# The hidden layer of a two-layer graph network: its up product as seven half-width products per pair of hidden blocks

## The reference, cut to what matters

```python
h = maximum(layernorm(x), 0);  x = x + L0_gnn_ref(h, W, src, dst, edge_weight)
h = maximum(layernorm(x), 0)
# second layer
h  = h + segment_sum(h[src], dst)            # N x 256
h1 = h @ W1 + b1                             # N x 1024, the "up product"
h1 = relu((h1 - mean) * rsqrt(var + 1e-5) * gamma + beta)
out = relu(h1 @ W2 + b2)                     # N x 256, the "down product"
x = x + out
```

## Time and profile before

| | |
|---|---|
| median of 3 runs | 3866.1 us (3864.36 to 3868.13) |
| the profiled execution: its own time | 3856.75 us |
| its span | 3854.9 us |
| TensorE, busy over the span | 3418.6 us, 17,108 matmuls |
| VectorE | 2279.5 us, 5,133 instructions |
| ScalarE | 2125.0 us, 3,435 instructions |
| GpSimd | 1155.8 us, 899 instructions |
| first up matmul of the node stage | at 1665.7 us |
| one full chunk of the node stage | 22.31 us |

### The profile page before, as it was taken

One profiled execution on the slowest core, in us unless ns is written; L12 is line 12 of the kernel. 1 busy time (PEld: TensorE's weight loads), 2 busy tenths in 40 slices (PEclk: granted clock), 3 DMA queues, 4 the chain that ended last, 5 costly groups with the idle time before them and its releaser, 6 DMA issues.

```text
span 3854.9 us, 57297 instructions
## 1 busy us (share of the span) xinstructions
PE 3418.6 (89%) x17108; PEld 2899.8 (75%) x17108; DVE 2279.5 (59%) x5133; ACT 2125.0 (55%) x3435; POOL 1155.8 (30%) x899
## 2 busy tenths in 40 slices
PE   0378887587877879999999999999999999999999
PEld 0367777576766657778888888888888888888888
DVE  0356665576565579955555555555555555555555
ACT  0255555323222279956666666666666666666665
POOL 6667777688888744400000000000000000000000
PEclk9888988788888889999999999999999999999999
DMA  9988877577777799933433433433333343343342
GB/s 343 338 201 192 191 191 141 140 169 163 157 161 154 169 319 378 363 120 113 125 116 111 125 118 109 124 121 109 121 124 109 116 129 109 115 130 109 114 125 69
DMA packets 305855, 619.83 MB, mean 161 GB/s; under 512 B 34997, under 2 KB 186800, under 8 KB 299856
## 3 DMA queue, kind: packets, MB, share of 16 engines
q1 hardware_dynamic: 229440, 515.46, 40.4%
q0 software_dynamic: 75264, 102.81, 15.6%
q10 hardware_dynamic: 1072, 0.76, 0.1%
...
## 4 chain that ended last, share of the span: by engine, by line
PE 63%; POOL 19%; DMA 8%; issue 7%; DVE 1%; ACT 1%; POOLq 0%; DVEq 0%; SPq 0%; ACTq 0%
PE ps_a L1303 28%; PE ps_b L1317 19%; PE ps_b L1318 10%; POOL x_table L554 7%; POOL agg_table L554 7%; POOL edge_tiles L544 4%; DMA x_table<-in_x 4%; PE ps_a L1261 3%; PE ps_a L1263 2%; DMA x_table<-edge_tiles,scatter_now 2%; PE ps_a L1262 2%; DMA agg_table<-edge_tiles,scatter_now 1%; POOL edge_ring L544 1%; DVE late_r L1039 0%; DMA edge_tiles<-x_table,gather_ids 0%
## 5 line engine op out<-in xcount | busy, mean ns | idle before, releaser
L1317 PE MATMUL ps_b<-w_hl,late_r 128*128 128x512 f32 x3128 | 1129.2, 397 | 0.0
L1145 DVE TENSOR_TENSOR late_r<-hid,late_r 128x512 fp32r<-128x512 f32 (+1 forms) x784 | 537.4, 685 | 813.6 <-ACT late_r L767 813.6
L762 ACT ACTIVATE hid<-ps_a,bn_bias,bn_scale 128x512 f32<-128x512 f32 (+1 forms) x784 | 608.8, 777 | 733.9 <-PE ps_a L1303 733.9
L1303 PE MATMUL ps_a<-late_r,w_hi 128*128 128x512 f32 x3136 | 983.5, 395 | 0.0
L1318 PE MATMUL ps_b<-w_hl,late_r 128*128 128x256 f32 x3128 | 877.6, 281 | 0.0
L1317 PEld LDWEIGHTS ps_b<-w_hl,late_r 128*128 128x128 f32 x3128 | 588.1, 188 | 137.9 <-issue 0.5
L1303 PEld LDWEIGHTS ps_a<-late_r,w_hi 128*128 128x128 f32 x3136 | 540.4, 188 | 107.9
L1303 PE MATMUL ps_a<-late_r,w_lo 128*128 128x512 f32 x1568 | 612.3, 390 | 0.0
L1318 PEld LDWEIGHTS ps_b<-w_hl,late_r 128*128 128x128 f32 x3128 | 591.2, 189 | 26.3
L767 ACT ACTIVATE late_r<-hid 128x512 fp32r<-128x512 f32 (+1 forms) x784 | 494.8, 631 | 71.7
L1231 PE MATMUL ps_b<-edge_tiles,edge_same 128*128 128x256 f32 x1568 | 408.2, 426 | 0.0
...
## 6 DMA issues: line engine op xcount, KB each, us to landing
x_rows<-x_table SPq DMA_DIRECT2D x291, 512.0 KB, 4.4
late<-agg_table SPq DMA_DIRECT2D x194, 512.0 KB, 5.8
...
hT_f<-hT_table SPq DMA_DIRECT2D x97, 512.0 KB, 3.7
out<-zeros SPq DMA_DIRECT2D x97, 512.0 KB, 6.7
...
```

The lines of the kernel that those rows point to most:

```text
L762: act.activation(hid[m % 2][:, 0:w].rearrange("p (r a b) -> p r a b", a=BANDS, b=SQUARE), by_row, ACT.Relu, scale=bn_scale[:, m:m + 1], bi ...
L1145: dve.tensor_tensor(hid_lo[m % 4][:, 0:w], hid[m % 2][:, 0:w], hid_hi[m % 4][:, 0:w].bitcast(F32), ALU.subtract).then_inc(hid_lo_ready, 1)
L1303: ins = pe.matmul(ps_a[:, 2 + m % 2, 0:w], w_part[:, kb, cols], h_part[:, kb * w:(kb + 1) * w], start=(t == 0), stop=(t == len(terms) - 1))
L1317: pe.matmul(ps_b[:, r, :], hid_hi[m % 4][:, cols], w2, start=(m == 0), stop=(m == MB - 1), skip_group_check=True)
```

## The change

The 1,024 hidden values are taken as 4 pairs of blocks. For a pair, the up product is a product of a 2 x 2 block matrix of weights (two hidden blocks by two feature blocks) with a 2 x 2 block matrix of rows (two feature blocks by two halves of 256 nodes). Instead of 8 block products it is formed from 7, in Winograd's form of Strassen's scheme: four sums of weight blocks (S1 to S4, made once, in the second edge stage) and four sums of row blocks (T1 to T4, made for every chunk).

- **TensorE.** 7 products x 3 terms = 21 matmuls of 256 columns per pair, 84 per chunk, in place of 48 matmuls of 512 columns. The down matmuls keep their shape and number in a full chunk, but are issued in 32 pieces of two, spread between the products by the strings in `ORDER`, and run 20 pieces behind (`LAG`). A group of nodes is now a band, so the last chunk has four groups of 96 nodes where it had three of 128.
- **ScalarE** copies products 1 and 5 out of their quarters of a bank (`take_p1_p5`, two instructions per pair). Its copy of the rows is split in two: three blocks (`take_hT`) and the four T blocks (`take_mixed`).
- **VectorE** adds product 5 to two sums in PSUM per pair (`add_p5_to_u2`, `add_p5_to_u3`, 256 columns each), and its `hT_low` is two instructions. It no longer copies the norm's constants.
- **GpSimd** forms T1 to T4 (`mix_h`, four instructions of 256 columns, all operands in SBUF) and copies the norm's constants. `mix_h` starts when the chunk's rows have landed, the second low part of the current chunk is made and the first half of the previous chunk's down sums is complete.
- **SyncE.** A chunk's result is stored in four DMAs of 128 KB with runs of 1 KB, and its residual rows are loaded again in four DMAs of the same form (`load_x1_out`). Order in `store`: four stores, four residual loads, the two row loads of a later chunk, then `turn_h` with its four stores and one load.
- `W1`'s split makes four sums, seven copies and seven subtractions of 512 columns.

The diff, cut to its core:

```diff
+        def quarters(i):
+            pair = ps_a[:, 2 * (i % 2):2 * (i % 2) + 2, :].rearrange("p t (v x) -> p (t v) x", v=2)
...
+            def store(n, s, k):
                 sp.wait_ge(out_ready, n + 1)
-                if load:
-                    load_main(n + LOADS, s)
-                sp.dma_start(chunk_of(out, n), tile_of(out_sb[s % 2], n)).then_inc(out_stored[s % 2], 16)
-                sp.wait_ge(out_stored[s % 2], 16 * turn_of(s, k) + 16)
+                for rows, parts, bands in band_rows(out, n):
+                    sp.dma_start(rows, out_sb[s % 2][parts, bands, :]).then_inc(out_stored[s % 2], 16)
+                if has(n, 2):
+                    load_x1_out(n + 2, s)
+                if has(n, 5):
+                    sp.wait_ge(h_ready, n + 4)
+                    load_main(n + 5, s + 5)
+                if has(n, 3):
+                    turn_h(n + 3)
...
+            def mix_h(n, after=None):
+                half = width(n) // 2
+                b12, b11, b22, b21 = (hT_f[:, q * half:(q + 1) * half] for q in range(4))
+                t1, t2, t3, t4 = (t_f[:, q * half:(q + 1) * half] for q in range(4))
+                pool.wait_ge(hT_loaded, 16 * n + 16)
+                if after is not None:
+                    pool.wait_ge(hid_lo_ready, MB * after + 2)
+                    if not is_first(after):
+                        pool.wait_ge(down_half, after)
+                if not is_first(n):
+                    pool.wait_ge(hT_lo_ready, 2 * n)
+                pool.tensor_tensor(t1, b12, b11, ALU.subtract).then_inc(t1_ready, 1)
+                pool.tensor_tensor(t3, b22, b12, ALU.subtract)
+                pool.wait_ge(t1_ready, n + 1)
+                pool.tensor_tensor(t2, b22, t1, ALU.subtract).then_inc(t2_ready, 1)
+                pool.wait_ge(t2_ready, n + 1)
+                pool.tensor_tensor(t4, b21, t2, ALU.subtract).then_inc(t_ready, 1)
+            def main(n, s, k):
+                if has(n, 1):
+                    mix_h(n + 1, after=n)
+                if has(n, 3):
+                    pick_norm(n + 3, (s + 1) % 2)
...
+            def take_p1_p5(n, i):
+                half = width(n) // 2
+                act.wait_ge(p1_p5_done, PAIRS * n + i + 1)
+                act.activation(quarters(i)[:, 2, 0:half], quarters(i)[:, 0, 0:half], ACT.Copy)
+                act.activation(p5_sb[i % 2][:, 0:half], quarters(i)[:, 1, 0:half], ACT.Copy).then_inc(p1_p5_taken, 1)
...
-                                      ALU.subtract).then_inc(w12_split, 1)
+                    chain.then(dve.tensor_tensor(w2_hl[:, :, 1, :], w2_f, w2_hl[:, :, 0, :].bitcast(F32), ALU.subtract))
+                    chain.wait()
+                    w1_block = w1_f.rearrange("p k (g h n) -> p k h g n", g=PAIRS, h=2)
+                    a11, a21, a12, a22 = (w1_block[:, kb, half, :, :] for kb in range(KB) for half in range(2))
+                    s1, s2, s3, s4 = (w1_mixed[:, f, :, :] for f in range(4))
+                    chain.then(dve.tensor_tensor(s1, a21, a22, ALU.add))
+                    chain.then(dve.tensor_tensor(s3, a11, a21, ALU.subtract))
+                    chain.wait()
+                    chain.then(dve.tensor_tensor(s2, s1, a11, ALU.subtract))
+                    chain.wait()
+                    chain.then(dve.tensor_tensor(s4, a12, s2, ALU.subtract))
+                    chain.wait()
+                    parts = ((A11, a11), (A12, a12), (A22, a22), (S1, s1), (S2, s2), (S3, s3), (S4, s4))
+                    for at, part in parts:
+                        chain.then(dve.tensor_copy(w1_hi[:, at, :, :], part))
+                    chain.wait()
+                    for at, part in parts:
+                        ins = dve.tensor_tensor(w1_lo[:, at, :, :], part, w1_hi[:, at, :, :].bitcast(F32), ALU.subtract)
+                    ins.then_inc(w12_split, 1)
                 passes = (0, (GROUPS - first - (AHEAD + 2)) // l.ring)[l.n]
...
+            def hT_low(n, s, mixed):
+                half = width(n) // 2
+                blocks = slice(T1 * half, H_PARTS * half) if mixed else slice(0, T1 * half)
+                whole = t_f[:, 0:4 * half] if mixed else hT_f[:, half:4 * half]
+                dve.wait_ge(hT_hi_ready, 2 * n + (2 if mixed else 1))
+                dve.scalar_tensor_tensor(hT_lo[s % 2][:, blocks], whole, 1.0, hT_hi[s % 2][:, blocks].bitcast(F32),
+                                         ALU.mult, ALU.subtract).then_inc(hT_lo_ready, 1)
...
+            def add_p5_to_u2(n, i):
+                half = width(n) // 2
+                dve.wait_ge(p1_p5_taken, PAIRS * n + i + 1)
+                dve.wait_ge(p6_done, PAIRS * n + i + 1)
+                dve.tensor_tensor(quarters(i)[:, 3, 0:half], quarters(i)[:, 2, 0:half], p5_sb[i % 2][:, 0:half], ALU.add).then_inc(u2_read, 1)
+            def add_p5_to_u3(n, i):
+                half = width(n) // 2
+                dve.wait_ge(up_done, MB * n + 2 * i + 1)
+                dve.tensor_tensor(quarters(i)[:, 1, 0:half], quarters(i)[:, 2, 0:half], p5_sb[i % 2][:, 0:half], ALU.add).then_inc(u3_read, 1)
...
+            def read_down(n, s, half):
+                p = width(n) // BANDS
+                bands = slice(2 * half, 2 * half + 2)
+                if half == 0:
+                    dve.wait_ge(out_retired, n + 1)
+                    dve.wait_ge(down_half, n + 1)
+                else:
+                    dve.wait_ge(down_done, MB * n + MB)
+                chain.then(dve.tensor_tensor(out_sb[s % 2][0:p, bands, :], ps_b[0:p, bands, 0:D],
+                                             b2_bc[0:p, :].rearrange("p (a d) -> p a d", a=1).to_broadcast([p, 2, D]), ALU.add))
+                chain.wait()
+                dve.tensor_tensor(out_sb[s % 2][0:p, bands, :], out_sb[s % 2][0:p, bands, :], ps_b[0:p, bands, D:2 * D],
...
-                for m in range(MB):
-                    dve.wait_ge(hid_hi_ready, MB * n + m + 1)
-                    if m >= 4 or not first:
-                        dve.wait_ge(down_done, MB * n + m - 3)
-                    dve.tensor_tensor(hid_lo[m % 4][:, 0:w], hid[m % 2][:, 0:w], hid_hi[m % 4][:, 0:w].bitcast(F32),
-                                      ALU.subtract).then_inc(hid_lo_ready, 1)
-                    if m == 0 and has(n, 1):
-                        turn_squares(*following(n, s, k))
-                    if m == 2 and not first:
-                        finish(n - 1, (s - 1) % LOADS)
-                    if m == 4 and has(n, 3):
-                        pick_norm(n + 3, (s + 1) % 2)
-                    if m == 6 and has(n, 1):
-                        hT_low(n + 1, s + 1)
-                    if m == 7 and has(n, 2):
-                        add_agg(*following(*following(n, s, k)))
+                    hidden_low(n - 1, 6)
+                add_p5_to_u3(n, 0)
+                if not first:
+                    hidden_low(n - 1, 7)
+                add_p5_to_u2(n, 1)
+                hidden_low(n, 0)
+                add_p5_to_u3(n, 1)
+                hidden_low(n, 1)
+                if not first:
+                    read_down(n - 1, s - 1, 0)
+                add_p5_to_u2(n, 2)
+                if not first:
+                    read_down(n - 1, s - 1, 1)
+                add_p5_to_u3(n, 2)
+                hidden_low(n, 2)
+                hidden_low(n, 3)
+                if has(n, 1):
+                    hT_low(n + 1, s + 1, False)
+                add_p5_to_u2(n, 3)
+                if not first:
+                    finish(*preceding(n, s, k))
+                if has(n, 1):
+                    hT_low(n + 1, s + 1, True)
+                hidden_low(n, 4)
+                add_p5_to_u3(n, 3)
+                if has(n, 2):
+                    add_agg(*after_next(n, s, k))
+                hidden_low(n, 5)
             add_agg(1, 1, 0)
...
+            def product(n, s, i, number):
+                weight, part, to, first = {1: (A11, B11, 0, True), 2: (A12, B21, 0, False), 3: (S4, B22, 3, False),
+                                           4: (A22, T4, 2, False), 5: (S1, T1, 1, True), 6: (S2, T2, 2, False),
+                                           7: (S3, T3, 2, False)}[number]
+                half = width(n) // 2
+                cols = slice(part * half, (part + 1) * half)
+                terms = ((w1_hi, hT_hi), (w1_hi, hT_lo), (w1_lo, hT_hi))
+                for t, (w_part, h_part) in enumerate(terms):
+                    ins = pe.matmul(quarters(i)[:, to, 0:half], w_part[:, weight, i, :], h_part[s % 2][:, cols],
+                                    start=(first and t == 0), stop=(t == len(terms) - 1), skip_group_check=True)
+                return ins
+            def p5(n, s, i):
+                if i == 0:
+                    pe.wait_ge(hT_lo_ready, 2 * n + 2)
+                if i >= 2 or not is_first(n):
+                    pe.wait_ge(hid_ready, MB * n + 2 * i - 2)
+                product(n, s, i, 5)
+            def p1(n, s, i):
```

(19 more changed lines are left out.)

395 lines of the change are left out of this document (246 added, 149 removed).

## The result

The changed kernel took **3851.65 us** (median of 5 runs, 3848.67 to 3852.33), the kernel before beside it 3866.1 (5 runs, 3863.6 to 3871.6): a ratio of 0.996, 95% interval 0.9949 to 0.9971. It is faster by 14.5 us, more than the 7.7 us that a measurement can tell, and lies within the range, but 63 us above the predicted 3789. The profiled execution took 3851.82 us, its span is 3850.0.

What follows compares the result with a forecast made beforehand. The prediction took TensorE's issue time in the node stage as the bound: -97 us there and +20 outside the loop turn 3856.75 into 3780, or 3789 us with 9.35 added for the median; range 3772 to 3892.

Steps and rivals of the forecast that it cites:

- TensorE per chunk: Node stage: 84 short matmuls replace 48 long ones, a chunk takes 21.3 us against 22.3, -97 us in all.
- The others keep up: Node stage: ScalarE at 17.8 us and VectorE at 16.9 both fit in a chunk of 21.3 us.
- rival "handovers": Node stage: ScalarE's PSUM copies cost as much as 512 columns, 0.8 us a chunk shows, near 3866 us; chance 0.06.
- The way of the rows: Node stage: turned rows land at 11.7 us, sums end at 14.7, ScalarE copies them at 16.4, 1.6 us left.
- The price of the sums: Node stage: GpSimd's four row sums take 0.75 us each, 3.0 us in all per chunk.
- Outside the loop: Second edge stage, start, first chunk, pieces after the last chunk, last chunk and end: +20 us together.
- Start: From the rows' landing to the first up matmul: four sums more, +3 us (2 to 5).
- first chunk, last chunk, drain and end: Node stage's edges: uncovered handovers +3 us, last chunk's narrow matmuls +4, remaining down pieces +1, final DMA issues and VectorE +3.
- The edge term of +6: Second edge stage: VectorE's weight split takes 5.9 us more and GpSimd has no lead left, +6 us (0 to 6.5).
- Sum: Whole kernel: -97 + 20 = -77 us, giving 3780 for the profiled execution and 3789 us for the median.
- The first one: Node stage: GpSimd's sums and VectorE's two-input work hold each other up, 0.5 us a chunk, 3838 us; chance 0.20.
- The second: Node stage, SyncE's queue: rows land at 13.3 us, sums end at 18.4, about 1.5 us show, 3934 us; chance 0.22.

Runs made afterwards that it cites:

- version that only writes: Changed kernel with GpSimd filling the sums' table with zeros instead of reading the rows, sums left out: 3787.04 us, ratio 0.978.
- the rows first: Changed kernel with SyncE issuing the turned rows' stores and load right behind the out stores, before residual and row loads: 3787.18 us, ratio 0.978.

## Why the prediction was right or wrong

- **TensorE per chunk: right.** 21.33 us in every version that doesn't stall, against 21.3. The 0.1 taken for handovers came to 0.13 (84 x 0.1191 + 11.2 = 21.2), and no idle time of TensorE is left in such a chunk. The 9.2 us for the up product that followed from the isolated gap of the Trainium skill ("TensorE: Matmul & The Clock Gate", "Back-to-back issue gap") would have made 20.4; no version has a mean chunk under 21.33.
- **The others keep up: right.** VectorE 16.27 us (16.9), ScalarE 16.52 (17.8), and no rival "handovers".
- **The way of the rows: wrong**, and this is the step that failed: "the rows land at about **11.7** us" and "That leaves 1.6 us" (1.7 by its own terms). Counted as the prediction counts, from the chunk's first product, what stands around it was right: the stores are issued at 2.2 us where TensorE never stands, without a queue the rows land at 10.0 (9.8), the gate opens at 11.1 (11.0), and ScalarE comes to its copy of the sums at 16.4 (16.4). The queue was wrong: behind the residual and row loads the rows land at 13.0 and not at 11.7 (version that only writes), since 7.1 us and not 5.8 pass from the first store's issue to the load's. The 0.4 us for 128 KB in runs of 1 KB stood on no row; the run length turned out to be the smaller part. Another 0.4 pass from the landing to GpSimd's first instruction, which the prediction put at nothing. So 3.0 us of sums would end at 16.4: the margin is 0.0 and not 1.6, with rows that scatter by 2 to 3 us from chunk to chunk.
- **The price of the sums: wrong with it.** They took 4.07 us and not 3.0, because so late they no longer stand beside readings of PSUM but beside `hidden_low`, `hT_low` and `finish`, which they stretch as well. VectorE then comes to the next transposition 1.96 us after the first product instead of 0.95, so the next rows land later still, at 13.9, and the sums end at 18.3. This last step is the one that costs: with late rows but without the stretching nothing is lost, and with stretching but early rows neither.
- **Outside the loop: half right.** Start: 20.9 us from the Gram copy to the first up product instead of 17.3 and 19.0 in the two traces of before, +2 to +4 for my +3 (20.0 to 22.9 in the other traces of the change). From the first up product to the end: 2189.2 and 2190.4 us before, 2103.6 with the rows first, 86 less. The loop alone gives 96 x 0.98 = 94, so first chunk, last chunk, drain and end cost 8 together; they were priced at 11. The edge term of +6 is wrong; it was hidden.
- **Sum.** Without late rows: -86 + 3 = -83, and 3871.5 - 3787.2 = 84 was measured. The changed kernel gives back 97 x 0.70 = 68 of it, which leaves 16, measured 14.5. That the result still lies within the stated range is owed to the range's width, not to the forecast, which allowed for no stall beyond 0.1 us a chunk.
- **Rivals.** The first one was the case, with its mechanism and place as described, 0.70 us a chunk where I had written 0.5, and 3838 us for it; it had 0.20. The second (rows too late, 3934) had the better times: rows at 13.3 (measured 13.0, and 13.9 with VectorE behind), sums to 18.4 (18.3), and it named the queue of SyncE rightly. Its price of 0.6 us per 128 KB in 1 KB runs was about a third of the reason (16 of 46 us), and its cost was wrong: of 2.0 us of lateness about 1.5 were to show, and 0.70 did. What parted the forecast from rival 1 was the margin alone, and that hung on one estimate of the queue, 1.3 us off, and a start delay of 0.4 left out.
